# Two-part scores of two heads on halves of the array, gathered diagonals and one pool of banks, in a post-LN layer with attention and routed experts

## The reference

```python
scores = jnp.einsum('bhqd,bhkd->bhqk', q, k) * scale
mask = jnp.triu(jnp.full((t, t), NEG, jnp.float32), k=1)
attn = jax.nn.softmax(scores + mask, axis=-1)
out = jnp.einsum('bhqk,bhkd->bhqd', attn, v)
...
x = _layernorm(x + attention(x))
scores = jnp.einsum('bh,he->be', x.mean(axis=1), Wr) + br
top1 = jnp.argmax(scores, axis=-1)
h = jax.nn.relu(jnp.einsum('bnh,bhf->bnf', x, W1[top1]) + b1[top1][:, None, :])
x = _layernorm(x + jnp.einsum('bnf,bfh->bnh', h, W2[top1]) + b2[top1][:, None, :])
```

## Time and profile before

| | |
|---|---|
| median of 3 runs (lowest, highest) | 890.5 us (888.81, 890.85) |
| profiled execution, its own time | 887.39 us |
| its span, first to last instruction | 885.7 us |
| mean granted TensorE clock | 0.952 of 2.4 GHz |
| busy in the span: PE, DVE, ACT, POOL | 790.1, 692.9, 433.1, 390.3 us |
| matmuls, DVE, ACT, POOL instructions | 5232, 2094, 808, 733 |
| DMA | 49.96 MB, 32.7% of the 16 engines' span |

### The profile page before, as it was taken

The page is one execution under the profiler, slowest core; times in us unless marked ns, Lnnn a source line. Parts: engine busy times, 40 slices in busy tenths (PEclk is TensorE's granted clock), DMA queues, the critical chain, the costliest instruction groups (busy, mean ns, idle before and its releaser), DMA issues. The chain is left out here.

```text
span 885.7 us, 15643 instructions
## 1 busy us (share of the span) xinstructions
PE 790.1 (89%) x5232; PEld 463.6 (52%) x5232; DVE 692.9 (78%) x2094; ACT 433.1 (49%) x808; POOL 390.3 (44%) x733
## 2 busy tenths in 40 slices
PE   3778999889999799999999999999988899994697
PEld 2414225224453475665653576666553466773696
DVE  6799888888888867788889987888978884447564
ACT  1003666636546537556356645654436646740441
POOL 9004315523272954526534973545465845132010
PEclk9758999989999989999999999999999999998799
DMA  3472660660436160240277260320376200000300
GB/s 107 49 94 90 81 73 4 72 74 3 56 73 98 61 84 16 36 52 15 61 122 100 76 85 1 57 43 4 78 114 103 63 14 2 15 14 12 102 24 26
DMA packets 44243, 49.96 MB, mean 56 GB/s; under 512 B 14722, under 2 KB 28802, under 8 KB 44162
## 3 DMA queue, kind: packets, MB, share of 16 engines
q1 hardware_dynamic: 44162, 48.95, 32.7%
HBM read 18.64 MB, written 4.19 MB: 26 GB/s over the span
## 5 line engine op out<-in xcount | busy, mean ns | idle before, releaser
L826 ACT ACTIVATE prob<-exp_ps 128x512 f32<-128x512 f32 x576 | 319.9, 597 | 257.4 <-PE exp_ps L452 253.9
L624 DVE CUSTOM_DVE_ANT_0 max_ps<-max_ps,causal 128x512 f32<-128x512 f32 (+3 forms) x512 | 237.7, 516 | 18.8 <-PE max_ps L440 17.9
L440 PE MATMUL max_ps<-stack_k,stack_q 96*128 96x512 bf16 (+3 forms) x768 | 218.7, 348 | 32.9 <-DVE partial_max L627 12.8
L452 PE MATMUL exp_ps<-stack_q,stack_k 128*128 128x512 bf16 (+3 forms) x768 | 195.8, 330 | 6.8 <-ACT prob L826 5.4
L890 POOL TENSOR_SCALAR_AFFINE_SELECT prob<-prob 128x128 f32<-128x128 f32 x512 | 141.1, 306 | 100.6 <-ACT prob L826 100.1
L627 DVE TENSOR_REDUCE partial_max<-max_ps 128x1 f32<-128x512 f32 x256 | 167.1, 681 | 21.3 <-PE max_ps L440 19.9
L468 PE MATMUL o_ps<-prob,v_ones 128*32 128x512 f32 (+3 forms) x1536 | 160.4, 497 | 0.6 <-POOL prob L890 0.5
L440 PEld LDWEIGHTS max_ps<-stack_k,stack_q 96*128 96x128 bf16 x768 | 60.8, 98 | 180.1 <-DVE partial_max L624 72.1
L452 PEld LDWEIGHTS exp_ps<-stack_q,stack_k 128*128 128x128 bf16 x768 | 66.8, 98 | 92.1 <-ACT prob L826 39.4
L544 PE MATMUL dense_ps<-x1T_hi,w_hi 128*128 128x256 f32 x256 | 85.5, 334 | 8.0 <-ACT w_hi L423 7.9
L560 PE MATMUL dense_ps<-w_hi,hidden_hi 128*128 128x256 f32 x256 | 81.8, 319 | 1.7 <-DVE x1T_lo L721 1.1
(11 more groups left out here) (98 smaller groups left out, 1078.4 us busy)
## 6 DMA issues: line engine op xcount, KB each, us to landing
stack_k<-parts SPq DMA_DIRECT2D x64, 96.0 KB, 2.8
stack_q<-parts SPq DMA_DIRECT2D x64, 96.0 KB, 3.1
stage<-in_w SPq DMA_DIRECT2D x24, 256.0 KB, 2.7
xT_sb<-in_xT SPq DMA_DIRECT2D x4, 1024.0 KB, 5.0
stack_k<-parts SPq DMA_DIRECT2D x64, 64.0 KB, 3.2
stack_q<-parts SPq DMA_DIRECT2D x64, 64.0 KB, 3.2
out<-ln_in SPq DMA_DIRECT2D x16, 256.0 KB, 2.2
x_sb<-in_x SPq DMA_DIRECT2D x3, 1024.0 KB, 5.5
```

Source lines behind the costliest of these rows:

```text
L440: done = engine.matmul(bank[:, at * P:(at + blocks) * P], stack_q[slot][0:ROWS, c, i * P:(i + 1) * P], stack_k[slot][0:ROWS, c, k0 * P:(k0 ...
L452: done = engine.matmul(bank[:, at * P:(at + blocks) * P], stack_k[slot][:, c, j * P:(j + 1) * P], stack_q[slot][:, c, q0 * P:(q0 + blocks) ...
L624: done = engine.tensor_tensor_reduce(src, src, causal[:, BANK - blocks * P:], 1.0, MASKED, ALU.add, ALU.max, dst)
L826: engine.activation(prob[n % P_RING][:, :], exp_ps[n % 2][:, :], ACT.Exp, scale=SCALE).then_inc(act_exp, 1)
```

## The change

Queries and keys are split in two float32r parts (rounded float32) in place of three bf16 parts, with three products, so that a head takes 48 rows of the array (64 with the two rows of the maxima and padding). Two heads share a stack (`stack_q`, `stack_k` of [128, T], 5 slots), one on rows 0 to 63 of the array and one on rows 64 to 127, and each step `m` or `e` computes a segment of both heads in turn into two neighbouring banks. DVE and ACT work on both banks in one instruction. There are half as many `m` and `e` steps (288 each). The 9 units of `m` of a pair of heads are 32 matmuls, those of `e` 24, together 28 pairs of segments (10 of 512 columns, 2 of 384, 10 of 256, 6 of 128).

The 8 diagonal blocks of a head are no longer masked in DVE's reduction: ACT copies them from PSUM to `diagonal` (`g`), POOL sets what lies above the diagonal to a large negative number (`k`), DVE reduces 8 blocks at once (`D`). Zeros in `prob` are set for two heads at once. The division is made on 32 by 32 blocks turned by DVE (`T`, reciprocal `i`, product `u`, turned back `V`); the copy, the two DMAs, the shuffle and the addition go. The epsilon and power of the layer norm go to POOL (`s`, `S`), most of its scaling too (`z`, `Z`). The mean for the router is taken by ACT's accumulator while it copies the transposed tokens; step `s` of PE goes. Expert weights are loaded into 8 buffers of their own (parts of `attn`, in the last sequence `prob`) in place of 2 shared ones. All of PSUM is one tensor of 8 banks, and a string `BANKS` says which bank each step takes. `wq`, `wk` are loaded from ACT's queue and `xT` in halves. All order strings are new.

```diff
 MAX_UNITS = [
-    [(4, 0, 4, 0)], [(5, 0, 4, 0)], [(6, 0, 4, 0)], [(7, 0, 4, 0)], [(3, 0, 4, 0)], [(7, 4, 4, 0)],
-    [(2, 0, 3, 0), (4, 4, 1, 3)], [(0, 0, 1, 0), (6, 4, 3, 1)], [(1, 0, 2, 0), (5, 4, 2, 2)],
+    [(0, 0, 1, 0), (2, 2, 1, 1), (4, 4, 1, 2), (6, 6, 1, 3)], [(1, 0, 2, 0), (3, 2, 2, 2)], [(5, 4, 2, 0), (7, 6, 2, 2)],
+    [(4, 0, 4, 0)], [(5, 0, 4, 0)], [(6, 0, 4, 0)], [(7, 0, 4, 0)], [(2, 0, 2, 0), (3, 0, 2, 2)],
+    [(6, 4, 2, 0), (7, 4, 2, 2)],
 ]
...
-        part_rest = sb("part_rest", [P, BANK])
-        stack_q = [sb(f"stack_q{i}", [P, G, T], BF16) for i in range(3)]
-        stack_k = [sb(f"stack_k{i}", [P, G, T], BF16) for i in range(3)]
+        parts = sb("parts", [P, 2, 2, T], F32R)
+        stack_q = [sb(f"stack_q{i}", [P, T], F32R) for i in range(SLOTS)]
+        stack_k = [sb(f"stack_k{i}", [P, T], F32R) for i in range(SLOTS)]
...
-        prob = [sb(f"prob{i}", [P, BANK]) for i in range(P_RING)]
+        neg_max = sb("neg_max", [G * C, 2, P], F32R)
+        diagonal = [sb(f"diagonal{i}", [P, 2, 4, P]) for i in range(2)]
+        prob = [sb(f"prob{i}", [P, 2, BANK]) for i in range(P_RING)]
+        turned = sb("turned", [P, BANK // 32, 32])
+        normal = sb("normal", [P, T // 32, 32])
...
-        max_ps = [ps(f"max_ps{i}") for i in range(2)]
-        exp_ps = [ps(f"exp_ps{i}") for i in range(2)]
-        dense_ps = [ps(f"dense_ps{i}") for i in range(2)]
-        o_ps = ps("o_ps", T)
+        ps = ctx.enter_context(nc.psum_tensor("ps", [P, 8, BANK], F32))
...
+        def two_banks(kind, n):
+            i, j = banks[kind, n]
+            return ps[:, i:j + 1, :]
...
-                    g, n = step // SLOTS, step % SLOTS
-                    c, u = n // UNITS, n % UNITS
-                    slot, bank = g % 3, max_ps[n % 2]
-                    pe.wait_ge(*fill_done(g, c))
-                    if step >= 2:
-                        pe.wait_ge(dve_max, step - 1)
-                    for s, (i, k0, blocks, at) in enumerate(MAX_UNITS[u]):
-                        done = engine.matmul(bank[:, at * P:(at + blocks) * P],
-                                             stack_q[slot][0:ROWS, c, i * P:(i + 1) * P],
-                                             stack_k[slot][0:ROWS, c, k0 * P:(k0 + blocks) * P], start=True, stop=True)
-                    done.then_inc(pe_max, 1)
+                    h, u = n // UNITS, n % UNITS
+                    slot, tile = h % SLOTS, two_banks("m", n)
+                    pe.wait_ge(*fill_done(h))
+                    for q, k0, blocks, at in MAX_UNITS[u]:
+                        for s in range(2):
+                            rows = slice(64 * s, 64 * s + ROWS)
+                            ends[s] = engine.matmul(tile[:, s, at * P:(at + blocks) * P],
+                                                 stack_q[slot][rows, q * P:(q + 1) * P],
+                                                 stack_k[slot][rows, k0 * P:(k0 + blocks) * P], start=True, stop=True)
+                    for s in range(2):
+                        ends[s].then_inc(pe_max, 1)
                 elif kind == "e":
...
                     for j, q0, blocks, at in EXP_UNITS[u]:
-                        done = engine.matmul(bank[:, at * P:(at + blocks) * P],
-                                             stack_k[slot][:, c, j * P:(j + 1) * P],
-                                             stack_q[slot][:, c, q0 * P:(q0 + blocks) * P], start=True, stop=True)
-                    done.then_inc(pe_pv, 1)
+                        for s in range(2):
+                            rows = slice(64 * s, 64 * s + 64)
+                            ends[s] = engine.matmul(tile[:, s, at * P:(at + blocks) * P],
+                                                 stack_k[slot][rows, j * P:(j + 1) * P],
...
                     engine.scalar_tensor_tensor(
-                        out=part_rest[:, :], in0=dense_ps[unit_at["q", n] % 2][:, :],
-                        scalar=bqk_sb[:, which, p % PAIRS:p % PAIRS + 1], in1=parts[:, which, 0, cols],
-                        op0=ALU.add, op1=ALU.subtract).then_inc(dve_rest, 1)
-                    dve.wait_ge(dve_rest, n + 1)
-                    engine.tensor_copy(parts[:, which, 1, cols], part_rest[:, :]).then_inc(dve_part, 1)
+                        out=parts[:, which, 1, cols], in0=bank("q", n), scalar=bqk_sb[:, which, p % PAIRS:p % PAIRS + 1],
+                        in1=parts[:, which, 0, cols].bitcast(F32), op0=ALU.add,
+                        op1=ALU.subtract).then_inc(dve_part, 1)
...
-                    for at, blocks, diagonal, column in TAKES[u]:
-                        src, dst = bank[:, at * P:(at + blocks) * P], partial_max[:, c, column:column + 1]
-                        if diagonal:
-                            done = engine.tensor_tensor_reduce(src, src, causal[:, BANK - blocks * P:], 1.0, MASKED,
-                                                               ALU.add, ALU.max, dst)
-                        else:
-                            done = engine.tensor_reduce(dst, src, AX_X, ALU.max)
+                        dve.wait_ge(act_diag, 3 * h + u + 1)
+                        src = tile.rearrange("p h (b k) -> p h b k", k=P)[:, :, 0::2, :]
+                        dst = to[:, :, 4 * u - 3:4 * u:2, 2]
+                    engine.tensor_reduce(dst, src, AX_X, ALU.max).then_inc(dve_max, 1)
+                elif kind == "D":
+                    to = partial_max[:, 2 * (h % 2):2 * (h % 2) + 2, k::2, 3]
+                    engine.tensor_reduce(to, diagonal[k][:, :, :, :], AX_X, ALU.max).then_inc(dve_diag, 1)
...
-                    engine.tensor_copy(neg_max[:, 1, :], neg_rest[:, :]).then_inc(dve_neg_mid, 1)
-                    dve.wait_ge(dve_neg_mid, n + 1)
-                    engine.tensor_tensor(neg_max[:, 2, :], neg_rest[:, :], neg_max[:, 1, :],
-                                         ALU.subtract).then_inc(dve_neg, 1)
+                    engine.scalar_tensor_tensor(out=neg_max[:, 1, :], in0=rows, scalar=-1.0,
+                                                in1=neg_max[:, 0, :].bitcast(F32), op0=ALU.mult,
+                                                op1=ALU.subtract).then_inc(dve_neg, 1)
...
-                    engine.stream_shuffle(inv_wide[:, :], inv_rows[:, half * BANK:(half + 1) * BANK],
-                                          mask).then_inc(dve_spread, 1)
+                    engine.transpose(turned[:, :, :].rearrange("p t c -> p (t c)"), bank("o", n)).then_inc(dve_turned, 1)
+                elif kind == "i":
+                    dve.wait_ge(dve_turned, n + 1)
+                    engine.reciprocal(inverse[:, :], turned[:, :, HD]).then_inc(dve_inv, 1)
+                    engine.transpose(attn[:, pair % PAIRS, half * BANK:(half + 1) * BANK],
+                                     normal[:, rows, :].rearrange("p t c -> p (t c)")).then_inc(dve_attn, 1)
...
-                    engine.activation(prob[n % P_RING][:, :], exp_ps[n % 2][:, :], ACT.Exp,
+                    engine.activation(prob[n % P_RING][:, :, :], two_banks("e", n), ACT.Exp,
+                    if u == 0:
+                        done = engine.copy(diagonal[0][:, :, :, :], tile)
+                    else:
+                        done = engine.copy(diagonal[1][:, :, 2 * u - 2:2 * u, :], tile[:, :, 1::2, :])
...
-            engine.memset(stack_q[0][:, :, :], 0.0).then_inc(s_open[0], 1)
-            for i in (1, 2):
-                engine.memset(stack_k[i][:, :, :], 1.0).then_inc(s_open[i], 1)
-                engine.memset(stack_q[i][:, :, :], 0.0).then_inc(s_open[i], 1)
...
+                    engine.affine_select(out=blocks, in_=blocks, compare_op=ALU.is_ge, fill=MASKED, base=0,
+                                         pattern=[[0, 8], [-1, P]], channel_multiplier=1).then_inc(pool_diag, 1)
...
-                    for dst, a in (
-                        (k[0:ROWS3, c, :], src[:, 1, :, :]),
-                        (q[0:ROWS3, c, :], src[:, 0, 0:1, :].broadcast_to([HD, 3, T])),
-                    ):
-                        engine.dma_start(dst, a).then_inc(s_fill[slot][c], DMA_DONE)
+                    for s in range(2):
+                        lane = (g % 2) * G + 2 * hp + s
+                        src = parts[lane * HD:(lane + 1) * HD, :, :, :].bitcast(F32)
+                        q, k = stack_q[slot][64 * s:64 * s + ROWS, :], stack_k[slot][64 * s:64 * s + ROWS, :]
+                        for dst, a in ((k[0:2 * HD, :], src[:, 1, :, :]),
+                                       (q[0:2 * HD, :], src[:, 0, 0:1, :].broadcast_to([HD, 2, T])),
+                                       (k[2 * HD:ROWS, :], src[:, 1, 0, :]),
+                                       (q[2 * HD:ROWS, :], src[:, 0, 1, :])):
+                            engine.dma_start(dst.bitcast(F32), a).then_inc(s_fill[slot], DMA_DONE)
...
-                    for i in range(PARTS):
```

(10 more changed lines are left out.)

## The result

The changed kernel takes 980.1 us, median of 4 runs (977.4 to 984.2), against 889.9 us of the kernel before on the same chip: 1.102 times as long, 95% interval 1.097 to 1.106. The forecast was 794 us with a range from 725 to 868. Some executions of e7, e8, e10 and e13 further down fell in a slower state with a lower granted clock, and the medians and ratios of all kernels leave such executions out.

What follows compares the result with a forecast made beforehand. The prediction took PE and DVE as both near their limit, DVE setting the pace while maxima are taken. Start 57, middle need 575, waits 65 and end 92 gave a 789 us span, 794 us forecast, range 725 to 868.

Steps and rivals of the forecast that it cites:

- The middle's waits: Between first `e` and last `p`: TensorE's waits fall from 100 to 65 us, since DVE has 20% less to do.
- the need that I subtracted, 612 us: Kernel before, first `e` to last `p`: PE's need put at 612 us, leaving 100 us as waits.
- The start: Up to the first `e`: first `m` at about 28 us, first `e` at 57 us, 17 us earlier than before.
- Change of array shape: Along PE's order: 366 new changes of shape at 0.07 us each add 26 us, bounds 0 and 51 us.
- The scores: Score matmuls on PE: 896 pairs of halves side by side take 209 us in place of 253, bounds 148 and 297.
- the first rival: Score matmuls: weight loads of the two halves overlap, scores 148 us, total 743 us; chance 0.2.
- PE's need of 682 us: TensorE over the whole kernel: scores, shape changes, `p`, experts and the rest need 682 us.
- DVE, ACT, POOL and the end: DVE falls from 693 to about 560 us, ACT busy about 490, POOL under 65%; stretch behind the last `p` 92 us.
- The slow one: Score matmuls: each change of half drains like a shape change, scores 422 us, total 973 us; chance 0.08.
- Waits staying at 100 us: Middle: maxima now pass ACT, POOL and DVE, so waits stay 100 us in place of 65, total 829; chance 0.2.

Runs made afterwards that it cites:

- e7: e1 with only the four fill transfers of a slot's upper head made, half of the data left out: 856.5 us, 0.960 of the kernel before.
- e8: Changed kernel with each group's maxima rows in four transfers of two rows instead of eight of one, still on SyncE: 953.3 us, 1.074 of the kernel before.
- e10: e9 with the maxima's rows in four transfers of two rows, 192 transfers instead of 384: 932.4 us, 1.052 of the kernel before.
- e13: e1 with all eight fill transfers of a slot, each for the first 512 tokens only: 878.6 us, 0.992 of the kernel before.
- e1: Changed kernel with the maxima's row transfers sent to output rows, so the second score product doesn't wait for them: 922.0 us, 1.038 of the kernel before.
- e2: Changed kernel with SyncE's order alone edited, maxima's rows ahead of stack fills they do not need: 976.7 us, 1.098 of the kernel before.
- e4: Changed kernel with streams of matmuls alone behind its last step, halves and full shapes, read for spacing and clock; its total time means nothing.
- e5: e1 with each half matmul of both score products run over all 128 rows: 941.0 us, 1.058 of the kernel before.
- e3: Changed kernel without GpSimd's 64 causal selects on the copied diagonal blocks: 980.3 us, 1.101 of the kernel before.
- e9: Changed kernel with a head's stack filled in two transfers instead of four, same bytes: 978.2 us, 1.102 of the kernel before.
- e6: Changed kernel with the maxima's rows in four transfers of two rows, issued by ScalarE ahead of each group's first exponential: 952.5 us, 1.071 of the kernel before.
- e11: e10 with the four transfers of a group's maxima issued by ScalarE: 953.4 us, 1.072 of the kernel before.

## Why the prediction was wrong, step by step

**The middle's waits (said: from 100 to 65 us) is the step that failed.** By the account, the middle of the kernel before has 667 us of work, 7 lost to the clock and 38 idle; that of the changed kernel 602, 68 and 138. Work fell by 65 us, waits and clock rose by 160. The 100 us were a remainder of my sum to begin with: TensorE is idle only 38 us there, and the need that I subtracted, 612 us, is below the 667 us of work. I took them all for waits for DVE's maxima and scaled them with DVE's load. DVE did get lighter, and the waits of weight loads for `partial_max` did fall (38.4 us over the whole span, against 57.3 and 51.0 in part of it). But what ended the waits of before says nothing of waits that it didn't have. I had the numbers: 128 rows of maxima in place of 48 and SyncE's queue named as what may be late, and the order with its few steps between `t` and `e`; I used them for the start alone. What the runs showed in place of DVE's maxima: waits for the rows of maxima, 65.7 us and up to 58 us of the time (e1), and for the stack fills that share SyncE's queue, of which half are worth 66 us (e7). That the fills come in bursts because stacks come free late is read from the trace (127.5 us of SyncE's waits against 21.2); no run has more stacks.

**The start (said: 57, was 74.4 us).** The first `m` came at 32.9 instead of 28. Four fills of eight transfers each, the last issued at 50.5, have landed only at 52.8, and ScalarE's fifth `q` waits 16.9 us for them with the diagonal copies of the second pair behind it. That is e2's mechanism. No run has an order that takes this `q` later, so its price is not known by itself.

**Change of array shape (said: 0.07 us each, 46 us in all).** The count was right, 664 in the trace. Each costs 0.093 us on the matmul before it and 0.105 on the first one behind it (0.025 into `p`), as the weights of the next shape are not loaded under the last matmul (e4). The changed kernel shows it around a visit to `p`:

```profile
189.48 0.50 PE L440 MATMUL ps<-stack_k,stack_q 48*128 48x512 f32 x2
189.82 0.40 PE L452 MATMUL ps<-stack_q,stack_k 64*128 64x512 f32 x2
190.15 1.06 PE L422 MATMUL ps<-prob,v_ones 128*32 128x512 f32 x8
191.14 0.50 PE L452 MATMUL ps<-stack_q,stack_k 64*128 64x512 f32 x2
```

`m` to `e` takes 0.34 us in place of 0.23, since it comes out of `p`; `e` to `p` 0.33, since it goes into it. 514 changes into other shapes at 0.2 us and 150 into 32 columns (`p` and `t`) at 0.12 are 121 us, 75 more than I had. I read the price from the length of a visit to `p`, which is 1.00 us in the changed kernel too: 0.07 us a change is only what falls inside the visit, and the part on the matmuls around it was missed.

**The scores (said: 209 us).** Without changes of shape a pair of halves costs 0.233 us with 512 columns, 0.228 with 384, 0.118 with 256, and 0.06 to 0.11 with 128; 896 pairs come to 145 us. That is the first rival's 148: the loads of the halves cost nothing on top. By the Trainium skill, TensorE: Matmul & The Clock Gate, section Packing small matmuls, loads overlap running matmuls where the row group differs; the trace agrees, with the starts of a pair 3 ns apart and 0.224 us from pair to pair. The 64 us that I was too high here and the 75 too low above cancel by luck, so PE's need of 682 us came out near for the wrong reasons.

**The clock was no term of mine.** I treated 0.95 as given. It cost 83 us in place of 25. With fewer waits it rises (0.87, then 0.89 in e1 and 0.92 in e7), so they take part in it; e5 shows that something in the half-shape scores does too, and e4's fall in a stream of changes makes the changes of shape likely, not shown.

**DVE, ACT, POOL and the end** were right: 581 us for 560, 466 for about 490, 370 under the bound, and 93.6 for 92.

**The rivals.** The slow one (973 us) had nearly the time and none of the mechanism: halves don't drain each other, 0.112 us a matmul and not 0.18. Waits staying at 100 us, through the diagonal's detour, was the right term with the wrong cause: e3 takes out the select and wins nothing, and TensorE's waits for ScalarE's copies are at most 15.4 us in the trace.

What stays open: e7's 856.5 us still is 62 above the forecast; the account gives 57 as lost to the clock and 716 as work, but how the clock's loss divides between shape changes and waits I can't say. Nor is it shown whether more stack slots or a longer lead would bring the changed kernel under before.

## What to carry to other kernels

A change that saves an engine's time can move the limit to a queue that no busy share shows: count the transfers at each turn of a dependent chain, what may stand in the queue ahead of them, and how many steps the order leaves between the last one issued and its first user. A queue can be late and yet stand idle: here it waited for buffers, then ran its fills in a burst just ahead of the rows. Merge small transfers (27 us here); merging large ones won nothing alone, and 21 us with the small ones merged too. Packing two small products side by side on the array pays half their streaming, but each step from one shape to another costs about as much as 512 columns, so run steps of one shape behind each other.

## What I had not expected of the hardware

- A change between half-row and full shape costs 0.205 us with float32r weights and 512 columns (e4; about 0.195 with 256), into 32-column weights 0.12 us (changed kernel).
- The granted clock fell to 1.2 GHz in a stream of matmuls with no other engine to wait for, 37 us into a pair of halves and a full matmul in turn (0.31 to 0.51 us a step at 1106 us in e4), and stayed at 2.4 GHz in 41 us of pairs of halves without a change.
- A fill of 128 or 256 KB holds SyncE's queue for 1.22 us in the mean (e9), one of 64 or 128 KB for 0.79 (changed kernel), one of 32 or 64 KB for 0.62 (e13), and a row of 4 KB for 0.64.
- Another engine's queue for the same row transfers won nothing (e6 952.5 against e8 953.3 us), and lost 21 us beside wide fills (e11 against e10).
